# A four-layer graph network on one core: Chebyshev scan factors in PSUM, carries added through TensorE, merged softmax steps

## Chip, core and metric

The kernel runs on one core of a Trainium2 chip. The metric is the device time of one execution in microseconds. Engines are named as in the profile: PE (TensorE), DVE (VectorE), ACT (ScalarE), POOL (GpSimd) and SP (SyncE); SBUF and PSUM are the on-chip memories, and PSUM has eight banks.

## The reference, cut to what matters

A graph has N = 3125 nodes with 32 features and E = 53125 edges, which come sorted by destination `dst`. Four layers follow each other, each with a residual and a layer norm:

```python
x = layernorm(x + gat_gru(x))      # softmax over the incoming edges, 4 heads, then a GRU gate
x = layernorm(x + cheb_gatv2(x))   # two Chebyshev steps, then a softmax with 1 head
x = layernorm(x + spline(x))       # 16 tent weights per edge
x = layernorm(x + agnn(x))         # cosine softmax with 1 head
```

A Chebyshev step is a sum over incoming edges, and a softmax layer a weighted one:

```python
m   = (x * Dinv[:, None])[src]                       # gather rows of the sources
agg = segment_sum(m, dst) * Dinv[:, None]
mx  = segment_max(e, dst)                            # softmax layers: e is a logit per edge
ex  = exp(e - mx[dst]); den = segment_sum(ex, dst)
out = segment_sum(feat[src] * (ex / den[dst])[:, None], dst)
```

So there are five passes over all edges that gather, weight and sum rows: `gat`, `cheb0`, `cheb1`, `gatv2` and `agnn` (the spline layer has a loop of its own).

## The kernel before

**Layout.** The edges lie as 125 partitions x 425 in their sorted order, and a pass goes through them in 17 chunks of 25 columns. The nodes lie as 125 partitions x 25. A node's edges can go on from one partition into the next; what a partition's last node hands on is called its carry.

**A chunk of a pass.** Each of a chunk's 25 columns needs 125 rows of a table. PE gathers 14 of the columns (12 in gat): `gather_rows` (L726) multiplies one-hot matrices with the table, in 15 matmuls a column (5 lots of sources x 3 bf16 parts), into PSUM, two columns to a bank (`columns_ps`). DVE takes the results out in two halves, columns 0 to 5 and 6 to 13 (`take_half`): for each half five copies under a mask (L1149), each with a small `memset` of a tile `idle` ahead of it (L1148). PE may not write a half again until DVE has taken it. DVE also makes four of the five one-hots of a chunk (L1121), ACT the fifth (L922, L925). POOL gathers the other 11 columns (13 in gat) from DRAM, one indirect DMA a column (`gather`, L613).

When both sets of rows are there, ACT turns them so that a feature's 25 edges lie side by side (L984 in the Chebyshev passes), and writes the keep factors, which are 0 where a new node begins and 1 elsewhere (L987; in a softmax pass they are rescaling factors, L957). DVE multiplies with the weights (softmax passes, L1453), adds the carry of the chunk before (L1545, or L1463 for each head) and runs one segmented scan over 32 features x 25 edges (`scan_chunk`, L1400: one scan for each head of 33 features in the softmax passes). ACT turns the scan back (L993, L965), and SP stores it to DRAM.

In a softmax pass DVE also keeps a running maximum: `brk` (L1430) marks the new nodes, a copy carries the last maximum (L1433), and one scan for each head (L1435) follows; then come two differences and a sum (L1440 to L1443) for ACT's exponentials (L954).

**The end of a pass.** POOL waits until the last scan is stored (`scan_stored`), and gathers `local`, the value where each partition's first node ends (`mend_get_i`). In `mend` PE multiplies the partitions' last values with `carry_qp` (L753; in softmax passes L759, L764 and L770 with maxima and rescaling between them), and DVE adds the carry to `local` (`finish_sums`, L1521, or L1509). POOL scatters the sum, `mended`, back into the stored scan (`mend_put_i`, L616), waits for it to land, and gathers the last row of every node, 25 gathers in five blocks (`agg<-...,end_i`). DVE works on each block of five nodes a partition as it lands (`block_in`).

**What orders the work.** Each engine runs its own program in order, and semaphores tie them. Most engines run chunks 2 to 13 in a loop (`chunks`, L308), while DVE's softmax passes are written out. After its five copies DVE signals `half_taken`; after a chunk's last half it signals `rows_filled` by way of one more memset (L1539), for which ACT waits at L984. SP's queue loads edges and stores scans, and some of its waits count the scatters (`scattered`). A long list of slots between DVE's steps (`more_hots`, `settle`) says where the one-hots go.

## Time and profile before

| | us |
|---|---|
| three runs | 2582.41, 2583.98, 2584.41 (median 2583.98) |
| profiled execution, its own time | 2578.79 |
| its span in the profile | 2577.1 |

| engine | busy share of the span |
|---|---|
| PE, matmuls / weight loads | 75% / 66% |
| DVE | 71% |
| POOL | 67% |
| ACT | 35% |

| stage | from - to (us of the span) |
|---|---|
| setup | 0 - 107 |
| gat's loop, then its pass end and the GRU | 107 - 462, 462 - 541 |
| cheb0's loop, then its pass end | 541 - 810, 810 - 861 |
| cheb1's loop, then its pass end and the products for gatv2 | 861 - 1129, 1129 - 1221 |
| gatv2's loop, then its pass end | 1221 - 1527, 1527 - 1614 |
| spline layer | 1614 - 2195 |
| agnn's products, loop and pass end | 2195 - 2241, 2241 - 2523, 2523 - 2577 |

TensorE's granted clock is 0.877 on the mean. The stages were read off the timelines: a loop ends about where the last scan is stored. No engine is busy throughout, and different engines end the stages; a stage's time has to be read from the waits in it. Idle time of an engine that nothing waits for costs nothing.

### The profile page before, as it was taken

What the parts mean: (1) busy time and instruction counts of PE and PEld (TensorE: products, weight loads), DVE (VectorE), ACT (ScalarE), POOL (GpSimd) and SP (SyncE); (2) the same over time, 40 slices, a digit from 0 to 9 for tenths busy, and PEclk for the clock granted to TensorE, in tenths of its full rate; (3) what the DMA queues carried; (4) which work ended last, traced back from release to release, by engine and by line L of the source; (5) the groups of instructions that cost most, each with busy time, mean ns of one, the idle gap of its engine ahead of it and who ended that gap; (6) DMA issues with size and microseconds to landing.
All of it is one profiled execution on the core that took longest, in us unless ns stands there. A gap on an engine that the chain in (4) does not pass through costs nothing.

```text
span 2577.1 us, 51563 instructions
## 1 busy us (share of the span) xinstructions
PE 1930.1 (75%) x20425; PEld 1694.0 (66%) x20425; DVE 1825.0 (71%) x4970; ACT 895.8 (35%) x872; POOL 1736.5 (67%) x1625
## 2 busy tenths in 40 slices
PE   2778777269994699947788947588788878589990
PEld 2777777269994699946788942355455545589990
DVE  7699998355553355533899854588888888699975
ACT  0377775325443144422344425000000000144542
POOL 6777774447775677765566842677777776567773
...
DMA packets 83703, 194.91 MB, mean 76 GB/s; under 512 B 30960, under 2 KB 49816, under 8 KB 79746
## 3 DMA queue, kind: packets, MB, share of 16 engines
q1 hardware_dynamic: 31650, 139.14, 15.1%
...
## 4 chain that ended last, share of the span: by engine, by line
POOL 38%; DVE 23%; issue 19%; PE 10%; ACT 6%; DMA 5%; DVEq 0%; POOLq 0%; ACTq 0%; SPq 0%
POOL edges_d L613 18%; POOL rows L613 16%; PE ps L726 7%; DVE edges_d L1400 5%; POOL agg L613 3%; DVE edges_d L1329 3%; ACT scan L965 3%; DVE edges_d L1453 2%; DVE bigT L1400 2%; PE ps L883 2%; POOL starts_dram L616 2%; ACT edges_d L950 1%; DVE agg L1121 1%; DVE smallT L1121 1%; DMA starts_dram<-scan 1%
## 5 line engine op out<-in xcount | busy, mean ns | idle before, releaser
L726 PE MATMUL ps<-nodes,edges_d 125*128 125x160 bf16 x7140 | 502.7, 234 | 80.4 <-DVE nodes L1371 49.7
L726 PEld LDWEIGHTS ps<-nodes,edges_d 125*128 125x128 bf16 x7140 | 500.1, 99 | 82.9 <-DVE nodes L1371 49.8
L613 POOL DMA_INDIRECT edges_d<-tab_y_dram,attr x425 | 429.8, 1011 | 180.2 <-issue 129.2
L613 POOL DMA_INDIRECT rows<-tab_cheb_dram,src_i x374 | 409.4, 1095 | 148.4 <-issue 113.4
L726 PE MATMUL ps<-nodes,aggn 125*128 125x180 bf16 (+2 forms) x3546 | 394.8, 244 | 120.0 <-DVE rows L1149 62.9
L783 PE MATMUL ps<-edges_d,scan 125*125 125x480 bf16 x1700 | 361.3, 369 | 108.3 <-DVE edges_d L1813 108.3
L1149 DVE COPY_PREDICATED rows<-picks,ps 125x192 f32<-125x192 uint16 (+4 forms) x880 | 352.4, 402 | 79.3 <-issue 39.6
L783 PEld LDWEIGHTS ps<-edges_d,scan 125*125 125x125 bf16 x1700 | 226.2, 136 | 244.6 <-DVE edges_d L1813 113.5
L726 PE MATMUL ps<-nodes,agg 125*128 125x180 bf16 (+2 forms) x3564 | 336.0, 243 | 63.6 <-DVE rows L1149 63.6
L726 PEld LDWEIGHTS ps<-nodes,aggn 125*128 125x128 bf16 x3546 | 292.0, 101 | 126.5 <-issue 64.1
L726 PEld LDWEIGHTS ps<-nodes,agg 125*128 125x128 bf16 x3564 | 283.4, 101 | 69.5 <-DVE rows L1149 56.7
L613 POOL DMA_INDIRECT rows<-tab_dram,src_i x209 | 247.4, 1184 | 86.2 <-issue 59.1
L613 POOL DMA_INDIRECT rows<-tab_fsrc_dram,src_i x176 | 203.8, 1158 | 85.2 <-issue 50.6
L613 POOL DMA_INDIRECT rows<-tab_x_dram,src_i x176 | 195.3, 1109 | 70.3 <-issue 51.2
L1071 ACT ACTIVATE agg<-prod 125x160 bf16<-125x160 f32 x85 | 28.6, 337 | 543.1 <-DVE prod L1802 543.1
L726 PE MATMUL ps<-nodes,smallT 125*128 125x160 bf16 (+1 forms) x2214 | 202.8, 238 | 0.0
L984 ACT ACTIVATE bigT<-rows 125x800 f32<-125x800 f32 x34 | 54.2, 1593 | 331.0 <-DMA rows<-tab_cheb_dram,src_i 183.5
L726 PEld LDWEIGHTS ps<-nodes,smallT 125*128 125x128 bf16 x2214 | 169.0, 100 | 0.0
L1791 DVE TENSOR_TENSOR edges_d<-edges_d 125x640 f32<-125x640 f32 x85 | 71.0, 835 | 127.1 <-DMA edges_d<-tab_y_dram,attr 127.1
L1787 DVE TENSOR_SCALAR scan<-nodes,codes 125x625 bf16<-125x625 f16 x340 | 144.4, 441 | 0.0
L950 ACT ACTIVATE bigT<-rows 125x800 f32<-125x800 f32 x34 | 56.4, 1658 | 230.7 <-DVE rows L1149 225.6
L616 POOL DMA_INDIRECT starts_dram<-scat,start_i x75 | 77.8, 1038 | 78.6 <-DVE scat L1855 28.0
...
## 6 DMA issues: line engine op xcount, KB each, us to landing
...
edges_d<-tab_y_dram,attr POOLq DMA_INDIRECT x425, 2.6
...
```

The lines of the kernel that those rows point to most:

```text
L613: pool.indirect_dma_start(o, None, table, bass.IndirectOffsetOnAxis(index, 0)).then_inc(s, SLOT)
L616: pool.indirect_dma_start(table, bass.IndirectOffsetOnAxis(index, 0), rows_, None, bounds_check=last, oob_is_err=False).then_inc(scattered ...
L726: ins = pe.matmul(columns_ps[:, i, 0:PICKS * w], hots_[b][lot][:, i * NP:i * NP + P], parts_[:, part, at:at + PICKS * w], start=(lot == 0 ...
L783: ins = pe.matmul(ps[0:NP, lot, 0:PICKS * 3 * D], lot_hots[c][:, t, lot, :], picked[c][:, t, :, :].rearrange("p k c -> p (k c)"), start=(b ...
L950: nc.scalar.activation(z[b][:, at:at + D, :], r[:, :, 0:D].rearrange("p t f -> p f t"), ACT.Copy).then_inc(rows_flipped, 1)
L965: nc.scalar.activation(to, of, ACT.Copy).then_inc(rows_turned, 1)
L984: nc.scalar.activation(z[b], rows[0:NP, b, 0:L * D].rearrange("p (t c) -> p c t", c=D), ACT.Copy).then_inc(rows_used, 1)
L1149: ins = vec.copy_predicated(to[:, cols[0]:cols[-1] + 1, 0:w], over(picks[:, b, pick, cols[0]:cols[-1] + 1], w), columns_ps[0:NP, cols[0]:c ...
L1329: ins = vec.tensor_tensor_scan(ed[:, t0:t1, c], same_ps[:, t0:t1], ed[:, t0:t1, c], ed[:, t0 - 1, c:c + 1] if i else 0.0, ALU.mult, ALU.add)
L1400: ins = vec.tensor_tensor_scan(flat, keep[:, c:c + width, :].rearrange("p c t -> p (c t)"), flat, 0.0, ALU.mult, ALU.add)
L1787: vec.tensor_scalar(lot_hots[c][:, t, :, :].rearrange("p l c -> p (l c)"), nodes16[:, 0:LOTS * NP], codes[:, c, t:t + 1], None, ALU.is_equal)
L1791: vec.tensor_tensor(slot, slot, over(basis[:, bass.ds(t0 + c * LS, LS), :], D), ALU.mult)\
```

## The change

- **Chebyshev passes.** The keep factors no longer lie in SBUF but in PSUM banks 6 and 7 (`keeps_ps`), half of the features in each; ACT writes them in two activations, and DVE scans in two scans of 16 x 25 = 400 elements (`scan_sums`). To make room, PE's first half (six columns) lies three columns to a bank in banks 0 and 1 (`tight_ps`), the other eight two to a bank in banks 2 to 5. Matmuls and copies read their places from `column_ps` and `half_ps`.
- **Pass ends of cheb0, cheb1, gatv2 and agnn.** The scatter of `mended` goes, with the waits around it. The end rows are gathered straight behind the stored scan (in gatv2 and agnn behind the fetch of `local`, which stays for its maximum). The carry is added to the gathered rows: DVE spreads it over a partition's node columns (`carry_to_nodes`: one product of 25 x c elements), three f32 matmuls with `first_row_of` bring it to the right partition in PSUM banks 3 to 5, and `block_in` adds it to each block. In gatv2 and agnn the rows are rescaled first by factors for each node (`node_keep`, ten small operations), so a block takes four more operations. gat keeps its scatter.
- **Softmax passes.** All heads share one maximum scan, with a padded first element for each head; gat's four carry operations become two; the memsets of `idle` ahead of the copies go.
- **Setup.** An iota on POOL and some dozen small DVE operations make `first_row_of` and `first_col_of`; `no_carry_pq` is made at each pass end; `shift` moves into `bigT`. Counts of semaphores follow (SP waits for 2J+1 and 3J+1 scatters instead of 2J+3, 3J+4 and 3J+5).

The core of the diff (counts, tile declarations and renamed views are left out):

```diff
+        def mend_rows(c):
+            return tab[0:NP, :, :].rearrange("p j c -> p (j c)")[:, 0:J * c].rearrange("p (j c) -> p j c", c=c)
+        def mend_ps(m, c):
+            return ps[0:NP, 3 + m // 2, m % 2 * LS * c:(m % 2 + 1) * LS * c].rearrange("p (j c) -> p j c", c=c)
...
+        tight_ps = ps[:, 0:2, 0:3 * PICKS * D].rearrange("p b (s c) -> p b s c", s=3)
+        def column_ps(name, i):
+            if name not in ("cheb0", "cheb1"):
+                return columns_ps[:, i, 0:PICKS * GATHERED[name]]
+            if i < 6:
+                return tight_ps[:, i // 3, i % 3, :]
+            return columns_ps[:, i - 2, 0:PICKS * D]
+        def half_ps(name, half, cols, pick):
+            w = GATHERED[name]
+            if name not in ("cheb0", "cheb1"):
+                return columns_ps[0:NP, cols[0]:cols[-1] + 1, pick * w:(pick + 1) * w]
+            if half:
+                return columns_ps[0:NP, cols[0] - 2:cols[-1] - 1, pick * w:(pick + 1) * w]
+            return tight_ps[0:NP, :, :, pick * w:(pick + 1) * w]
+        HALF_D = D // 2
+        keeps_ps = [ps[0:NP, 6 + i, 0:HALF_D * L].rearrange("p (c t) -> p c t", t=L) for i in range(2)]
...
+                    if heads:
+                        gather(local[:, 0:C], scan_dram, mend_get_i[:, 0:1], local_in)
+                    if heads > 1:
+                        pool.wait_ge(vec_for_pool, vec_pool.up())
+                        scatter(scan_dram, mend_put_i[:, 0:1], mended[:, 0:C], E - 1)
+                        pool.wait_ge(scattered, put.at())
...
-                                        ins = pe.matmul(columns_ps[:, i, 0:PICKS * w],
+                                        ins = pe.matmul(column_ps(name, i),
...
+                def carry_to_nodes(c):
+                    pe.wait_ge(vec_for_pe, operand.up())
+                    for at in range(0, J, 2 * LS):
+                        n = min(2 * LS, J - at) * c
+                        ins = pe.matmul(ps[0:NP, 3 + at // (2 * LS), 0:n], first_row_of[:, :],
+                                        tab[0:NP, :, :].rearrange("p j c -> p (j c)")[:, at * c:at * c + n],
+                                        start=True, stop=True)
+                    ins.then_inc(pe_for_vec, 1)
...
+                        carry_to_nodes(D)
...
+                    if heads == 1:
+                        carry_to_nodes(MC)
...
-                        nc.scalar.activation(keep[:, :, 1:L],
-                                             samec[:, b, 1:L].unsqueeze(1).broadcast_to([NP, D, L - 1]),
-                                             ACT.Copy).then_inc(act_for_vec, 1)
+                        for part in keeps_ps:
+                            ins = nc.scalar.activation(part[:, :, 1:L],
+                                                       samec[:, b, 1:L].unsqueeze(1).broadcast_to([NP, HALF_D, L - 1]),
+                                                       ACT.Copy)
+                        ins.then_inc(act_for_vec, 1)
...
-                        vec.memset(idle[:, half * 8 + pick:half * 8 + pick + 1], 0.0)
-                        ins = vec.copy_predicated(to[:, cols[0]:cols[-1] + 1, 0:w],
-                                                  over(picks[:, b, pick, cols[0]:cols[-1] + 1], w),
-                                                  columns_ps[0:NP, cols[0]:cols[-1] + 1, pick * w:(pick + 1) * w])
+                        if name in ("cheb0", "cheb1"):
+                            vec.memset(idle[:, half * 8 + pick:half * 8 + pick + 1], 0.0)
+                        taken = to[:, cols[0]:cols[-1] + 1, 0:w]
+                        mask = picks[:, b, pick, cols[0]:cols[-1] + 1]
+                        if name in ("cheb0", "cheb1") and not half:
+                            taken = taken.rearrange("p (b s) c -> p b s c", s=3)
+                            mask = mask.rearrange("p (b s) -> p b s", s=3)
+                        ins = vec.copy_predicated(taken, over(mask, w), half_ps(name, half, cols, pick))
...
+                row_, col_, later = (place_of[:, i:i + 1] for i in range(3))
+                steps = cross[:, 0:NP]
+                again = cross[:, NP:2 * NP]
+                vec.tensor_scalar(row_, ends[:, 0:1], 1.0 / J, -(J // 2) / J, ALU.mult, ALU.add).then_inc(vec_done, 1)
+                settle()
...
+                vec.tensor_scalar(first_row_of[:, :], steps, row_, later, ALU.is_equal, ALU.mult)
+                vec.tensor_scalar(first_col_of[:, :], steps[:, 0:J], col_, None, ALU.is_equal)
...
+                def scan_sums(z, b):
+                    for i, part in enumerate(keeps_ps):
+                        flat = z[b][:, i * HALF_D:(i + 1) * HALF_D, :].rearrange("p c t -> p (c t)")
+                        ins = vec.tensor_tensor_scan(flat, part.rearrange("p c t -> p (c t)"), flat,
                                                      0.0, ALU.mult, ALU.add)
...
-                        vec.tensor_scalar(brk[:, :], same[:, bass.ds(t0, L)], -1.0, BIG, ALU.add, ALU.mult)
+                        vec.tensor_scalar(brk[:, 0:heads, 1:L + 1], same[:, t0:t0 + L].unsqueeze(1)
+                                          .broadcast_to([NP, heads, L]), -1.0, BIG, ALU.add, ALU.mult)
+                        vec.tensor_copy(padded_logit[:, 0:heads, 0:1], mrun[:, 1 - b, 0:heads, L:L + 1])
                         logits(r, t0)
-                        vec.tensor_copy(mrun[:, b, 0:heads, 0:1], mrun[:, 1 - b, 0:heads, L:L + 1])
-                        for h in range(heads):
-                            ins = vec.tensor_tensor_scan(mrun[:, b, h, 1:L + 1], brk[:, :], logit[:, h, :],
-                                                         mrun[:, 1 - b, h, L:L + 1], ALU.add, ALU.max)
-                        ins.then_inc(vec_done, 1)
+                        vec.tensor_tensor_scan(mrun[:, b, 0:heads, :].rearrange("p h t -> p (h t)"),
+                                               brk[:, 0:heads, :].rearrange("p h t -> p (h t)"),
+                                               padded_logit[:, 0:heads, :].rearrange("p h t -> p (h t)"),
+                                               0.0, ALU.add, ALU.max).then_inc(vec_done, 1)
...
-                        for h in range(heads):
-                            one_head = slice(h * HG, (h + 1) * HG)
-                            ins = vec.scalar_tensor_tensor(z[b][:, one_head, 0], z[1 - b][:, one_head, L - 1],
-                                                           rw[:, b, 0, h, 0:1], z[b][:, one_head, 0],
-                                                           ALU.mult, ALU.add)
-                        ins.then_inc(vec_done, 1)
+                        if heads == 1:
+                            vec.scalar_tensor_tensor(z[b][:, :, 0], z[1 - b][:, :, L - 1], rw[:, b, 0, 0, 0:1],
+                                                     z[b][:, :, 0], ALU.mult, ALU.add).then_inc(vec_done, 1)
+                        else:
+                            carried = mended[0:NP, 0:heads * HG].rearrange("p (h g) -> p h g", h=heads)
+                            vec.tensor_tensor(carried, z[1 - b][:, :, L - 1].rearrange("p (h g) -> p h g", h=heads),
+                                              over(rw[:, b, 0, 0:heads, 0], HG), ALU.mult).then_inc(vec_done, 1)
+                            settle()
+                            vec.tensor_tensor(zh[:, :, :, 0], zh[:, :, :, 0], carried, ALU.add).then_inc(vec_done, 1)
...
+                    if heads == 1:
+                        vec.tensor_copy(mended[0:NP, 0:HG], ps[0:NP, 6, 0:HG]).then_inc(vec_done, 1)
+                        settle()
+                        carry_to_nodes(mended[0:NP, 0:MC], MC)
+                        for m in range(J // LS):
+                            made = mend_ps(m, MC)
+                            vec.tensor_scalar(node_keep[:, 0, m * LS:(m + 1) * LS], made[:, :, HG + 2], -1.0, 1.0,
+                                              ALU.mult, ALU.add).then_inc(vec_done, 1)
+                        own.up(J // LS - 1)
+                        settle()
+                        for m in range(J // LS):
+                            js = slice(m * LS, (m + 1) * LS)
+                            vec.tensor_tensor(node_keep[:, 1, js], node_keep[:, 0, js], mend_ps(m, MC)[:, :, HG],
+                                              ALU.add).then_inc(vec_done, 1)
+                        own.up(J // LS - 1)
+                        settle()
+                        return
...
+                def carry_to_nodes(carry, c):
+                    vec.tensor_tensor(mend_rows(c), over(first_col_of[:, :], c),
+                                      carry.unsqueeze(1).broadcast_to([NP, J, c]), ALU.mult).then_inc(vec_for_pe, 1)
+                    vec.wait_ge(pe_for_vec, pe_n.up())
+                def block_in(m, heads=None):
                     vec.wait_ge(agg_in[m], agg_n.at())
+                    js = slice(m * LS, (m + 1) * LS)
+                    if heads == 0:
+                        vec.tensor_tensor(agg[0:NP, js, 0:D], agg[0:NP, js, 0:D], mend_ps(m, D), ALU.add)\
+                            .then_inc(vec_done, 1)
+                        settle()
+                    if heads == 1:
+                        vec.tensor_tensor(agg[0:NP, js, 0:HG], agg[0:NP, js, 0:HG], over(node_keep[:, 1, js], HG),
+                                          ALU.mult)
+                        vec.tensor_tensor(agg[0:NP, js, HG], agg[0:NP, js, HG], node_keep[:, 0, js], ALU.mult)\
+                            .then_inc(vec_done, 1)
+                        settle()
+                        vec.tensor_tensor(agg[0:NP, js, 0:HG], agg[0:NP, js, 0:HG], mend_ps(m, MC)[:, :, 0:HG], ALU.add)
+                        vec.tensor_tensor(agg[0:NP, js, HG], agg[0:NP, js, HG], mend_ps(m, MC)[:, :, HG + 1], ALU.add)\
+                            .then_inc(vec_done, 1)
+                        settle()
                 def finish_sums():
                     vec.wait_ge(pe_for_vec, pe_n.up())
-                    vec.wait_ge(local_in, local_n.up(SLOT))
-                    vec.tensor_tensor(mended[0:NP, 0:D], local[0:NP, 0:D], ps[0:NP, 6, 0:D], ALU.add)\
-                        .then_inc(vec_for_pool, 1)
+                    carry_to_nodes(ps[0:NP, 6, 0:D], D)
...
-                        scan_chunk(z, keep, b)
+                        scan_sums(z, b)
```

## Rows read from the trace of the kernel before

**Rows 1.** PE's timeline in cheb0's loop: start, us, instructions [idle before <-releaser]

```profile
541.91 162.75 PE L726 MATMUL ps<-nodes,edges_d 125*128 125x160 bf16 x2310 [21.35 <-issue]
705.59 14.70 PE L726 MATMUL ps<-nodes,edges_d 125*128 125x160 bf16 x210 [0.92 <-DVE rows L1149]
...
768.55 30.85 PE L726 MATMUL ps<-nodes,edges_d 125*128 125x160 bf16 x420 [2.09 <-DVE rows L1149]
```

**Rows 2.** PE's timeline in cheb1's loop, first and last of seven gaps

```profile
1008.61 14.70 PE L726 MATMUL ps<-nodes,edges_d 125*128 125x160 bf16 x210 [0.19 <-DVE rows L1149]
...
1100.79 14.68 PE L726 MATMUL ps<-nodes,edges_d 125*128 125x160 bf16 x210 [0.54 <-DVE rows L1149]
```

**Rows 3.** Groups by line and form: busy us, mean ns | idle before, releaser

```profile
L613 POOL DMA_INDIRECT rows<-tab_cheb_dram,src_i x374 | 409.4, 1095 | 148.4 <-issue 113.4 <-DMA tab_cheb_dram<-tab 34.9
...
L1716 DVE TENSOR_TENSOR prod<-prod,ps 125x800 f32<-125x800 f32 x17 | 16.8, 986 | 0.6
L1710 DVE TENSOR_TENSOR prod<-rows,edges_d 125x800 f32<-125x800 f32 x17 | 16.7, 983 | 0.0
```

**Rows 4.** Timelines of DVE and POOL at gatv2's start

```profile
1229.02 6.66 DVE L1329 TENSOR_TENSOR_SCAN edges_d<-ps,edges_d 125x75 f32<-125x75 f32 x32
...
1232.22 0.94 POOL L613 DMA_INDIRECT rows<-tab_fsrc_dram,src_i  x1 [0.30 <-issue]
```

**Rows 5.** Timelines of DVE and POOL, one cheb0 chunk; the last gather is cheb1's

```profile
559.59 0.44 DVE L1149 COPY_PREDICATED rows<-picks,ps 125x256 f32<-125x256 uint16 x1
...
566.74 1.82 DVE L1400 TENSOR_TENSOR_SCAN bigT<-bigT 125x800 f32<-125x800 f32 x1
...
566.99 2.32 POOL L613 DMA_INDIRECT rows<-tab_cheb_dram,src_i  x1 [0.30 <-issue]
...
570.13 0.37 DVE L1149 COPY_PREDICATED rows<-picks,ps 125x192 f32<-125x192 uint16 x1
...
1112.25 1.42 POOL L613 DMA_INDIRECT rows<-tab_cheb_dram,src_i  x1 [0.30 <-issue]
```

**Rows 6.** Timelines of DVE, ACT and POOL at the end of cheb0

```profile
801.96 0.06 DVE L1539 MEMSET idle<- 125x1 f32 x1
804.38 1.55 ACT L984 ACTIVATE bigT<-rows 125x800 f32<-125x800 f32 x1 [7.93 <-DMA rows<-tab_cheb_dram,src_i]
813.98 0.94 POOL L613 DMA_INDIRECT local<-scanD_dram,mend_get_i  x1 [11.10 <-DMA scanD_dram<-scan]
...
820.77 1.07 POOL L613 DMA_INDIRECT agg<-scanD_dram,end_i  x1 [1.38 <-DMA scanD_dram<-mended,mend_put_i]
```

**Rows 7.** Timelines of ACT and POOL at the end of cheb1

```profile
1122.68 1.54 ACT L984 ACTIVATE bigT<-rows 125x800 f32<-125x800 f32 x1 [7.94 <-DMA rows<-tab_cheb_dram,src_i]
1131.52 0.94 POOL L613 DMA_INDIRECT local<-scanD_dram,mend_get_i  x1 [10.36 <-DMA scanD_dram<-scan]
...
1137.44 0.96 POOL L613 DMA_INDIRECT agg<-scanD_dram,end_i  x1 [1.37 <-DMA scanD_dram<-mended,mend_put_i]
```

**Rows 8.** Timelines of POOL and PE at the end of gatv2

```profile
1530.46 0.94 POOL L613 DMA_INDIRECT local<-scan_dram,mend_get_i  x1 [18.34 <-DMA scan_dram<-scan]
...
1539.32 0.97 POOL L613 DMA_INDIRECT agg<-scan_dram,end_i  x1 [1.44 <-DMA scan_dram<-mended,mend_put_i]
...
1556.87 7.25 PE L883 MATMUL ps<-w_spl,smallT 32*125 32x512 f32 x8 [5.05 <-ACT smallT L900]
```

**Rows 9.** DVE's timeline in one chunk of gat

```profile
298.38 3.68 DVE L1453 TENSOR_TENSOR edges_d<-edges_d,ps 125x800 f32<-125x800 f32 x4 [0.58 <-ACT rw L954]
...
302.27 0.91 DVE L1463 SCALAR_TENSOR_TENSOR edges_d<-edges_d,rw 125x33 f32<-125x33 f32 x4
```

**Rows 10.** DVE's timeline at the end of agnn

```profile
2531.16 0.19 DVE L1509 TENSOR_TENSOR mended<-mended,ps 125x33 f32<-125x33 f32 x1 [0.72 <-PE ps L770]
2542.05 0.16 DVE L1880 TENSOR_TENSOR nodew<-agg,nodew 125x5 f32<-125x5 f32 x1 [10.70 <-DMA agg<-scan_dram,end_i]
...
2574.12 0.32 DVE L1592 TENSOR_TENSOR X<-X,nodew 125x160 f32<-125x160 f32 x1
```

85 lines of the change are left out of this document (55 added, 30 removed).

## The prediction

> **What bounds the kernel now.** I read the chain of waits first: it passes from stage to stage through different engines, so each stage has to be costed by itself. Then I read timelines of every engine, one chunk and one pass end per stage.
>
> In the two Chebyshev loops PE gathers by one-hot matmuls without a pause at first (cheb0's first eleven chunks take 162.75 us, 14.8 each); then it begins to wait for DVE's half-takes, in five gaps in cheb0, the first 0.92 us and the last 2.09, and in seven in cheb1, from 0.19 to 0.54 [rows 1, 2]. What makes DVE late is POOL. It issues 11 gathers a chunk, 374 in both loops with a mean of 1095 ns [rows 3]; an undisturbed one takes 0.94, with 0.30 of issue in front [rows 4], so 0.155 x 374 = 58 us are excess. 35 of the long gathers fall on a DVE scan, the first and the last shown: one begun just after a scan of 1.82 us takes 2.32 [rows 5]. Read one by one, those 35 hold 14.0 us of excess in cheb0 and 11.8 in cheb1; nearly all the rest falls beside the one-hot instructions, which stay. At the end of cheb0 DVE has taken its last half at 802.02, but ACT starts only at 804.38, on POOL's last rows [rows 6].
>
> At the pass ends POOL's 25 end-row gathers (1.25 us each) are the longest item. They begin only after fetch, mend, scatter-back and landing: 6.8 us after the fetch could have begun in cheb0 (813.98 to 820.77), 5.9 in cheb1, 8.9 in gatv2 [rows 6 to 8].
>
> In the gat loop DVE's weighted rows, scans and then ACT's copies form one closed ring: DVE waits 0.58 us for ACT's exponentials in a chunk [rows 9].
>
> **The change, part by part.**
>
> *Scan factors in PSUM.* While DVE ran 32 scans with one operand in PSUM for 6.66 us, POOL's gathers kept 0.94 [rows 4]. So I take off the whole scan excess: POOL's last rows come at 804.38 - 14.0 = 790.4 in cheb0 and at 1122.68 - 11.8 = 1110.9 in cheb1 [rows 6, 7]. PE's gaps then go: cheb0's add up to 5.1 us, and after the last, 420 matmuls took 30.85 instead of 2 x 14.70, 1.45 more; PE ends at 799.40 - 6.6 = 792.8 [rows 1]. DVE's last half ends 2.6 us behind PE (802.02 against 799.40) [rows 1, 6], so ACT starts at 795.4 instead of 804.38: 9.0 us. In cheb1 the gaps are 4.2 us; PE ends at 1111.3, ACT starts at 1113.9 instead of 1122.68: 8.8 us [rows 2, 7]. Late next is PE itself, at 14.6 to 14.8 us a chunk; POOL's 11 x 1.245 and 0.87 of stalls on one-hots make 14.6, just as long, so nothing beyond this is to be had.
>
> The new scan pair: 32 scans of 75 elements in 6.66 us are 2.8 ns an element [rows 4]; 800 in 1.82 are 2.3 [rows 5]. So 1.8 to 2.2 us; I take 2.0, since a larger scan spreads its fixed part. ACT's two half copies instead of one I put at 0.15 more (0 to 0.3). Both lie beside PE inside a loop: DVE's chain from the last half to the next half taken goes from 559.59 to 570.50, 10.9 us of PE's 14.7 [rows 1, 5]. At each loop's end they show, 0.3 us a pass. Net **-8.7 and -8.5**. Bounds: 0 (the scans hold POOL as before) and -9.0, -8.8.
>
> The tight layout of PE's first half changes no matmul. The split copies move the same elements; 0 to 0.1 us a piece, inside the 3.8 us of slack.
>
> *Carries through PE, cheb0 and cheb1.* The end-row gathers start when the scan is stored: 6.8 and 5.9 us earlier. The carry (one DVE product of 800, three f32 matmuls) runs while POOL gathers for 25 x 1.25 = 31 us. Its PE price: 4 products of 512 columns took 7.25 us, 3.5 ns a column [rows 8], so 800 cost 2.8, ready before the first five end rows. DVE adds one 160-element sum a block, 0.32 (the last of [rows 10]) and a gap, 0.4; one is exposed, behind the last block. **-6.4 and -5.5**; bounds 0.4 either way. Nothing queues behind POOL's dropped wait but these gathers.
>
> *Carries, gatv2 and agnn.* The local fetch stays (it gives the local maximum), the scatter goes: gathers start 1.25 us behind the fetch, at 1531.7 instead of 1539.3 [rows 8], 7.6 earlier; agnn is alike. But DVE gets a longer way to its first block. In agnn: the mended row at 2531.16 + 0.19, a product of 900 (0.98 for 800 [rows 3], so 1.1), 900 f32 columns (3.2), ten factors of five elements (0.06 to 0.16 each, 1.1), with gaps: 2537.0 instead of 2542.05, so 5.05 earlier [rows 10]. Each block then gets two 165-element and two 5-element operations, 0.95 us. agnn's blocks are already DVE's bound: from 2542.05 to 2574.44 five take 6.5 us each, over the 6.24 that five gathers need [rows 10]. All five additions count: -5.05 + 4.75 = **-0.3**. In gatv2 the same steps bring the first block 5.2 to 5.5 us earlier; PE's spline products, which wait through ACT's copy for the second block, start as much before 1556.87 [rows 8]; the fourth block, with one addition of 0.95 more ahead of it, leaves **-4.6**. Bounds: gatv2 -7.6 to 0, agnn -5 to +3.
>
> *Merged softmax steps.* In gat's ring only one piece changes: four carries of 0.91 us with gap become two of 0.29 with a wait between, 0.65 against 0.94 [rows 9]: 0.29 x 17 = **-4.9**. The merged maximum scan, the wider break row and the dropped memsets lie in the time in which DVE waits for ACT anyway: nothing. Bounds 0 and -6. In gatv2 and agnn a memset of 0.06 us (one like it: the first of [rows 6]) goes before each of ten copies a chunk; it lies inside the copy before it, so I take 0; were each worth its 0.06 in some 20 chunks that DVE bounds, 12.
>
> *Setup.* A dozen small DVE operations, some 2 us, stand before the counting; PE's first matmul waits for the zero-fill of a table and its last one-hot, so they are covered. If that cover were gone, +2. I take 0.
>
> **Sum**: -8.7 - 6.4 - 8.5 - 5.5 - 4.6 - 0.3 - 4.9 = -38.9, say 39 us, against a profiled span of 2577.1 (own time 2578.79, 5.2 under the median of the runs). Set against the median: 2583.98 - 39 = **2545 us**.
>
> One rule speaks against the change. The product of gatv2's logits that reads PSUM took 986 ns at 800 elements, the one before it out of SBUF 983 [rows 3]: 3 ns. The Trainium skill's VectorE: DVE Perf Modes (its section on the TRN2 errata) gives a fixed part of 120 cycles for a PSUM source against 58 for SBUF, an estimated 0.065 us for each new PSUM reader. By it the twenty or so new readers of the agnn tail and a few in the others would cost some 2.5 us, and the sum would be 2547.5; the row says it would not.
>
> **Rivals.** (1) *The scans go on holding POOL*, because what delays a gather is not the factors' place. Then both loops stay as they are and 39 - 17.2 = 21.8 remain: 2562. For it: the scans of rows 4 step through their tile with a stride, the new ones run contiguously. Against it: every one of their neighbours stayed near 0.94. A page would have it so: the Trainium skill's SBUF — State Buffer (Who interferes with whom) infers that a two-input DVE operation takes only the read interface while a DMA's descriptors need the write interface, by which such a scan would not stall a gather at all, and its place could not matter. The trace does not agree: 2.32 us on a scan [rows 5]. 8%.
> (2) *The carry chain becomes the bound of the tails.* If the carry's matmuls and node factors take twice my 5.4 us, gatv2 and agnn start their blocks later than reckoned, 0.8 and +5.1 instead of -4.6 and -0.3: 2555. For it: the tails are DVE-bound already. Against: the f32 price is measured. 8%.
> (3) *Slower:* the DVE chain takes PE's place in the Chebyshev loops, because scans or copies with PSUM are slow. A chunk now lasts 15.1 us on the mean (541.91 to 799.40, 17 of them); the other parts save 21.8, so this decides from 34 chunks x 0.64, a chunk of 15.8, which means a chain of 10.9 + 4.9. ACT's factor copy and the scan, some 2.7 now, would have to triple: 16.4 a chunk, +44 - 21.8, 2606. Against: rows 4 price the scan 20% up at most. 4%.
> (4) *The carry brings nothing because POOL is not the gate of the pass ends*: then 24 of 39 remain: 2560. Against: DVE idles until the first end rows land [rows 10]. 3%.
>
> **The numbers.** Forecast 77%, rivals 8, 8, 4, 3. The forecast's own bounds reach from 2531 (memsets worth their length, parts at their better ends) to 2555; with rival 1, and setup uncovered, at 2564 the range is 2531 to 2564. 0.2%, 5.2 us, is about what a measurement can tell from no change. Faster 92%; same 4% (the loops worse by what rival 3 needs to break even); slower 4%.
>
> **What would show it.** Chebyshev gathers that fall on scans at 0.94 instead of 1.4 to 2.3, and a mean near 1.02; PE gapless to the end of both loops; end-row gathers directly behind the stored scan; agnn's blocks at 7.5 us instead of 6.5; gat's chunk shorter by 0.3. Wrong would be: gathers still stretched; gaps in PE on DVE's halves; blocks that wait for the carry's matmuls for more than 3 us.

## The result, and the profile after

The changed kernel takes 2538.99 us (median; 2537.42 to 2542.16), against 2583.19 for the kernel before (four runs of each; the three runs shown ahead of the prediction are among them): a ratio of 0.9832 with a 95% interval of 0.9815 to 0.9849, or 44 us. Its profiled execution took 2538.81 us with a span of 2537.1, 40.0 us under the span of before.

From the page of the changed kernel, the span, the busy times and the engines' shares of the chain of waits:

```profile
span 2537.1 us, 51142 instructions
PE 1942.4 (77%) x20449; PEld 1701.2 (67%) x20449; DVE 1836.8 (72%) x4471; ACT 899.3 (35%) x906; POOL 1704.3 (67%) x1620
...
PE 28%; POOL 25%; DVE 24%; issue 13%; ACT 6%; DMA 4%; ACTq 0%; POOLq 0%; DVEq 0%; SPq 0%
```

The same line of the chain in the kernel before:

```profile
POOL 38%; DVE 23%; issue 19%; PE 10%; ACT 6%; DMA 5%; DVEq 0%; POOLq 0%; ACTq 0%; SPq 0%
```

POOL is busy 32 us less, the others about as long as before. What changed is who ends the stages: PE holds 28% of the chain instead of 10, POOL 25 instead of 38. To see where, I cut the span at instructions that both traces have: each pass's first gather matmul, and the first matmul of each pass end (the carry in the Chebyshev passes, the maxima in the softmax passes). The times are differences of such starts in PE's timelines. "Before, again" is the run e10_before_again below.

| stage (us) | before | before, again | after | measured change | predicted |
|---|---|---|---|---|---|
| setup | 73.1 | 72.7 | 72.7 | -0.4 | 0 |
| gat's loop | 383.6 | 384.0 | 382.8 | -0.7 | -4.9 |
| gat's end and the GRU | 85.3 | 84.9 | 84.8 | -0.4 | 0 |
| cheb0's loop | 268.7 | 267.3 | 257.8 | -10.9 | -8.7 |
| cheb0's end | 50.3 | 50.1 | 43.9 | -6.4 | -6.4 |
| cheb1's loop | 268.0 | 267.5 | 258.8 | -9.2 | -8.5 |
| cheb1's end | 69.5 | 69.6 | 64.2 | -5.3 | -5.5 |
| gatv2's loop | 327.6 | 327.6 | 322.9 | -4.7 | 0 |
| gatv2's end | 109.3 | 109.2 | 105.3 | -3.9 | -4.6 |
| spline layer | 585.4 | 591.5 | 589.5 | +4.1 | 0 |
| agnn's loop | 300.7 | 300.9 | 299.2 | -1.5 | 0 |
| agnn's end | 55.7 | 55.0 | 55.2 | -0.5 | -0.3 |

Between the two profiles of the kernel before, the spline layer moves by 6.1 us, cheb0's loop by 1.4, and no other stage by more than 0.7.

**The Chebyshev loops.** PE's timeline in cheb0 and cheb1, where before five and seven gaps stood [rows 1, 2], has one row for each loop:

```profile
540.36 248.72 PE L763 MATMUL ps<-nodes,edges_d 125*128 125x160 bf16 x3570 [21.36 <-issue]
...
842.09 249.72 PE L763 MATMUL ps<-nodes,edges_d 125*128 125x160 bf16 x3570 [39.14 <-DVE nodes L1448]
```

All 17 chunks run without a gap. Groups by line and form (busy us, mean ns | idle before, releaser):

```profile
L648 POOL DMA_INDIRECT rows<-tab_cheb_dram,src_i x374 | 382.0, 1022 | 148.8 <-issue 113.3 <-DMA tab_cheb_dram<-tab 35.4
...
L1488 DVE TENSOR_TENSOR_SCAN bigT<-ps,bigT 125x400 f32<-125x400 f32 x68 | 63.6, 977 | 1.2
...
L1034 ACT ACTIVATE bigT<-rows 125x800 f32<-125x800 f32 x34 | 54.3, 1596 | 302.8 <-DVE idle L1673 302.8
```

The gathers went from a mean of 1095 ns [rows 3] to 1022, and read one by one, none that falls on a scan is stretched any more: all that begin during one take 0.94 or 0.95 us. What excess is left lies beside the one-hots (L1121 before, L1173 after), which read one tensor and one column out of SBUF: 60 gathers that begin during one take more than 1.0 us, 28 us over 0.943 in both loops together, where it was 29 before. Two scans of 400 take 1.87 us where one of 800 took 1.82 [rows 5]. ACT now waits only for DVE's report that the last half is taken (L1673), and no longer for POOL's rows.

**The pass ends.** The end of cheb0 after the change, timelines of ACT, PE, POOL and DVE in order of time (start, us, instruction [idle before <-releaser]):

```profile
791.79 1.56 ACT L1034 ACTIVATE bigT<-rows 125x800 f32<-125x800 f32 x1 [8.04 <-DVE idle L1673]
...
799.92 3.03 PE L786 MATMUL ps<-tab,first_row_of 125*125 125x320 f32 x6 [1.15 <-DVE tab L1630]
801.39 0.94 POOL L648 DMA_INDIRECT agg<-scanD_dram,end_i  x1 [14.60 <-DMA scanD_dram<-scan]
...
809.09 0.32 DVE L1639 TENSOR_TENSOR agg<-agg,ps 125x160 f32<-125x160 f32 x1 [0.90 <-DMA agg<-scanD_dram,end_i]
```

The end rows' gathers are released by the stored scan itself and no longer by the scattered sum [rows 6]. The carry is through PE at 802.95, before the first five end rows have come, and each addition waits for its rows. In agnn the order is the other way round (the last row is the fifth block's):

```profile
2487.59 0.94 POOL L648 DMA_INDIRECT agg<-scan_dram,end_i  x1 [0.30 <-issue]
...
2493.47 3.36 PE L786 MATMUL ps<-tab,first_row_of 125*125 125x360 f32 x6 [1.42 <-DVE tab L1630]
2496.87 0.44 DVE L1614 TENSOR_SCALAR diag<-ps 125x5 f32<-125x5 f32 x5 [3.46 <-PE ps L786]
2497.35 0.44 DVE L1620 TENSOR_TENSOR diag<-diag,ps 125x5 f32<-125x5 f32 x5
2497.82 0.33 DVE L1643 TENSOR_TENSOR agg<-agg,diag 125x165 f32<-125x165 f32 x1
...
2527.19 0.33 DVE L1643 TENSOR_TENSOR agg<-agg,diag 125x165 f32<-125x165 f32 x1
```

The first block is not released by a DMA: its last row has landed at 2495.70, and DVE comes to it straight from the carry, after 3.46 us of waiting for PE and 0.95 of node factors. The blocks then follow each other every 7.34 us on the mean (2497.82 to 2527.19, four times), where it was 6.50.

### The profile page after: what moved, and what is told of

It reads as the page before. It is cut to its first block, busy times and chain, and to the rows that moved or that the text cites. A ratio compares the mean times of both kernels' runs of the same rounds, so it can differ in the third digit from the quotient of the medians.

```text
span 2537.1 us, 51142 instructions
## 1 busy us (share of the span) xinstructions
PE 1942.4 (77%) x20449; PEld 1701.2 (67%) x20449; DVE 1836.8 (72%) x4471; ACT 899.3 (35%) x906; POOL 1704.3 (67%) x1620
## 4 chain that ended last, share of the span: by engine, by line
PE 28%; POOL 25%; DVE 24%; issue 13%; ACT 6%; DMA 4%; ACTq 0%; POOLq 0%; DVEq 0%; SPq 0%
PE ps L763 25%; POOL edges_d L648 18%; DVE edges_d L1479 5%; POOL rows L648 3%; DVE rows L1207 3%; DVE edges_d L1406 3%; ACT scan L1015 3%; POOL agg L648 2%; DVE edges_d L1542 2%; PE ps L933 2%; POOL starts_dram L651 2%; DVE bigT L1479 1%; ACT edges_d L1000 1%; DVE agg L1173 1%; DMA starts_dram<-scan 1%
## 5 line engine op out<-in xcount | busy, mean ns | idle before, releaser
L648 POOL DMA_INDIRECT rows<-tab_cheb_dram,src_i x374 | 382.0, 1022 | 148.8 <-issue 113.3
## 6 DMA issues: line engine op xcount, KB each, us to landing
starts_dram<-scan SPq DMA_DIRECT2D x2, 3400.0 KB, 13.9
```

Source lines behind the costliest of these rows:

```text
L648: pool.indirect_dma_start(o, None, table, bass.IndirectOffsetOnAxis(index, 0)).then_inc(s, SLOT)
```

## The experiments

Each is the changed kernel with one edit, if nothing else is said; loops and ends are cut as in the table above. The diffs show the heart of an edit; "..." marks what is left out. The kernel before, run beside each group of experiments, had medians between 2582.84 and 2585.15 us, so times less than 3 us apart are not told apart here.

**e1_sbuf_factors and e2_one_sbuf_scan: what freed POOL?** The factors' place and the length of the scan changed together, so each needs a run of its own. e1 puts the factors back into SBUF and keeps the two scans:

```diff
-                    for i, part in enumerate(keeps_ps):
+                    for i, part in enumerate([keep[:, i * HALF_D:(i + 1) * HALF_D, :] for i in range(2)]):
```

(the same for ACT's two activations and the first column's memset). e2 has one activation and one scan of 800 as well:

```diff
-                        scan_sums(z, b)
+                        scan_chunk(z, keep, b)
```

> The changed kernel with its keep factors in SBUF again; the two scans of 400, ACT's two activations and the tight layout stay. Theory (what held POOL is that both operands of the scan lie in SBUF): both Chebyshev loops, from the first gather matmul to the carry matmul, go back from 257.8 and 258.8 us to about 268 each, gathers on scans take 1.4 to 2.3 us again, the time is about 2560 us (+20). Rival (two shorter scans let POOL through, wherever the factors lie): the loops stay at 258 to 260, at most +3 us.

> As e1_sbuf_factors, but with one scan of 800 and one activation as in the kernel before; only the tight layout of PE's columns is left of this part. Theory: within 3 us of e1_sbuf_factors, about 2560 us, loops of 268 us, so that the layout is worth nothing by itself. Rival (the split or the layout carries part of the gain): the two kernels differ by over 5 us, or the loops stay clearly under 268.

**e8_psum_one_scan** is the fourth corner: the factors in PSUM, as 800 elements in a row over banks 6 and 7, and one scan:

```diff
-                    for i, part in enumerate(keeps_ps):
-                        flat = z[b][:, i * HALF_D:(i + 1) * HALF_D, :].rearrange("p c t -> p (c t)")
-                        ins = vec.tensor_tensor_scan(flat, part.rearrange("p c t -> p (c t)"), flat,
...
+                    flat = z[b].rearrange("p c t -> p (c t)")
+                    ins = vec.tensor_tensor_scan(flat, keep_flat, flat, 0.0, ALU.mult, ALU.add)
```

> The changed kernel with its factors in PSUM, but as 800 elements in a row over both banks, read by one scan as long as that of the kernel before. Theory (a PSUM operand lets POOL through however long the scan): gathers on scans stay at 0.94 us, the loops at 258 to 259 us, time within 3 us of the changed kernel. Rival (only the length of a scan counts): gathers on scans at 1.4 to 2.3 us and loops of 268 us each, time about 2559 us.

| | one scan of 800 | two scans of 400 |
|---|---|---|
| factors in SBUF | e2: loops 268.9 and 268.3, 2561.25 us | e1: loops 258.9 and 258.6, 2542.28 us |
| factors in PSUM | e8: loops 257.7 and 259.0, 2542.72 us | changed kernel: 257.8 and 258.8, 2538.99 us |

The Chebyshev gathers and scans in e1, e2 and e8, groups by line and form, with the line of e1 for ACT's wait:

```profile
L648 POOL DMA_INDIRECT rows<-tab_cheb_dram,src_i x374 | 389.1, 1040 | 149.2 <-issue 113.4 <-DMA tab_cheb_dram<-tab 35.4 <-DMA scanD_dram<-scan 0.3
...
L1488 DVE TENSOR_TENSOR_SCAN bigT<-bigT 125x400 f32<-125x400 f32 x68 | 63.7, 978 | 1.2
...
L1034 ACT ACTIVATE bigT<-rows 125x800 f32<-125x800 f32 x34 | 54.3, 1597 | 303.5 <-DVE idle L1673 289.6 <-DMA rows<-tab_cheb_dram,src_i 13.9
```

```profile
L648 POOL DMA_INDIRECT rows<-tab_cheb_dram,src_i x374 | 410.3, 1097 | 149.0 <-issue 113.1 <-DMA tab_cheb_dram<-tab 35.5 <-DMA scanD_dram<-scan 0.3
...
L1477 DVE TENSOR_TENSOR_SCAN bigT<-bigT 125x800 f32<-125x800 f32 x34 | 62.0, 1825 | 1.2
```

```profile
L650 POOL DMA_INDIRECT rows<-tab_cheb_dram,src_i x374 | 383.3, 1025 | 148.6 <-issue 113.1 <-DMA tab_cheb_dram<-tab 35.1 <-DMA scanD_dram<-scan 0.3
...
L1489 DVE TENSOR_TENSOR_SCAN bigT<-ps,bigT 125x800 f32<-125x800 f32 x34 | 62.0, 1823 | 1.3 <-DVE bigT L1679 0.2
```

My theory for e1 fell: the loops did not go back, and its rival had them right. e2 shows that the gain is in this part, and that the tight layout, which e2 keeps, is worth nothing by itself. e8 shows that the place in PSUM is enough: a scan as long as before leaves the gathers alone. And e1 shows that the split is enough for the time. One chunk of e1 and one of e2, timelines of DVE and POOL:

```profile
564.68 1.87 DVE L1488 TENSOR_TENSOR_SCAN bigT<-bigT 125x400 f32<-125x400 f32 x2
564.86 1.57 POOL L648 DMA_INDIRECT rows<-tab_cheb_dram,src_i  x1 [0.30 <-issue]
```

```profile
564.61 1.82 DVE L1477 TENSOR_TENSOR_SCAN bigT<-bigT 125x800 f32<-125x800 f32 x1
564.88 2.31 POOL L648 DMA_INDIRECT rows<-tab_cheb_dram,src_i  x1 [0.31 <-issue]
```

A gather that begins 0.2 to 0.3 us into the first scan takes 0.63 us more than 0.94 where the scans are halves, and 1.37 where it is one. Read one by one, it is held to the end of the scan in which it begins: in the kernel before, in e2 and in e1 32 gathers each begin during a scan, and every one of them ends 0.75 us behind that scan's end. So in e1 gathers are still stretched, by 3.7 and 2.6 us a loop instead of 14.0 and 11.8, but POOL then needs 11 x (1.040 + 0.303) = 14.8 us a chunk, close to PE's 14.6. PE's timeline in e1 has no gap in either loop; only ACT waits 13.9 us for POOL's rows, which it does not in the changed kernel. The two means do the same work twice here. Whether the 3 to 4 us between e1 or e8 and the changed kernel (for e8 under 3 were expected) are theirs stays open: the spline stage, in which they do not differ, is 2.5 and 1.1 us longer in their profiles.

**e3_scatter_back** has the pass ends of before in cheb0, cheb1, gatv2 and agnn:

```diff
-                    if heads:
-                        gather(local[:, 0:C], scan_dram, mend_get_i[:, 0:1], local_in)
-                    if heads > 1:
-                        pool.wait_ge(vec_for_pool, vec_pool.up())
...
+                    gather(local[:, 0:C], scan_dram, mend_get_i[:, 0:1], local_in)
+                    pool.wait_ge(vec_for_pool, vec_pool.up())
+                    scatter(scan_dram, mend_put_i[:, 0:1], mended[:, 0:C], E - 1)
+                    pool.wait_ge(scattered, put.at())
```

> The changed kernel with the pass ends of before in cheb0, cheb1, gatv2 and agnn: fetch, scatter, landing, then end rows. Theory: the ends go back to 50.3, 69.5, 109.3 and 55.7 us, together +16 us, about 2555 us, and nothing else moves. Rival (the ends had another gate, and the gain there comes from something else): under +8 us.

Measured: 2557.41 us, and ends of 50.4, 69.3, 109.5 and 55.0 us. The first three are back where they were, together 15.8 us; agnn's, which the change had moved by 0.5, stays. Nothing else moved by more than the spline stage does between profiles. The carries are worth what the ends show.

**e4_max_scans, e5_memsets, e6_four_carries, e11_old_steps: the softmax steps, one by one and together.** e4 has a maximum scan for each head again, e5 a memset ahead of every copy, e6 gat's four carries, e11 all three. gatv2 and agnn have one head, so they have one scan either way; what e4 moves there is the small copy ahead of it.

```diff
-                        vec.tensor_tensor_scan(mrun[:, b, 0:heads, :].rearrange("p h t -> p (h t)"),
...
+                        for h in range(heads):
+                            ins = vec.tensor_tensor_scan(mrun[:, b, h, 1:L + 1], brk1, logit[:, h, :],
+                                                         mrun[:, 1 - b, h, L:L + 1], ALU.add, ALU.max)
```

```diff
-                        if name in ("cheb0", "cheb1"):
+                        if True:
                             vec.memset(idle[:, half * 8 + pick:half * 8 + pick + 1], 0.0)
```

```diff
-                        if heads == 1:
-                            vec.scalar_tensor_tensor(z[b][:, :, 0], z[1 - b][:, :, L - 1], rw[:, b, 0, 0, 0:1],
...
+                        for h in range(heads):
+                            one_head = slice(h * HG, (h + 1) * HG)
+                            ins = vec.scalar_tensor_tensor(z[b][:, one_head, 0], z[1 - b][:, one_head, L - 1],
...
```

> The changed kernel with one maximum scan for each head and the narrow break row, as before; carries and memsets stay as changed. Theory (gat is a ring of DVE's weighted rows, scans and ACT; gatv2 and agnn are mostly bound by DVE): gat's loop within 1 us, with DVE's wait for the exponentials down from 19.6 to about 13 us; gatv2's loop +1 to +2.5, agnn's 0 to +2; time +1 to +4 us. Rival (gat is bound by all that DVE does): gat's loop +6 us, 0.35 a chunk.

> The changed kernel with a memset of idle ahead of each of the ten copies of a chunk in the softmax passes too. Theory (gatv2's loop, which got 4.7 us shorter and of which the maximum scan gives back 1.7, is bound by DVE, and each memset delays the copy behind it by 10 ns or more): gatv2's loop +2 to +3 us, agnn's +0 to +3, gat's +0 to +2; time +2 to +7 us. Rival (a memset lies inside the copy before it): all three loops within 1 us.

> The changed kernel with gat's four carry operations of 33 elements instead of the two of 132. Theory (the two take 0.41 and 0.43 us with a wait between, the four 0.91 together, so the ring is as long as before): gat's loop within 1 us of 382.8, time within 3 us of the changed kernel. Rival (two operations are shorter by 0.29 us in the ring, as was reckoned): gat's loop +4.9 us.

> The changed kernel with all softmax steps as before: maximum scans for each head, four carries in gat, memsets ahead of all copies. Theory (together they are worth what gatv2's loop shows, each of them little): gatv2's loop back to 326 to 328 us, agnn's to 300 to 302, gat's 383 to 385; time +5 to +9 us on the changed kernel. Rival (gatv2's gain has another cause, such as the pass end of cheb1 ahead of it): gatv2's loop stays at 323 to 325.

| | gat's loop | gatv2's loop | agnn's loop | time |
|---|---|---|---|---|
| changed kernel | 382.8 | 322.9 | 299.2 | 2538.99 |
| e4_max_scans | 384.1 | 324.6 | 300.8 | 2544.88 |
| e5_memsets | 383.5 | 323.1 | 300.6 | 2542.81 |
| e6_four_carries | 382.7 | 323.5 | 299.0 | 2540.96 |
| e11_old_steps | 385.5 | 326.9 | 300.9 | 2548.15 |

Two expectations failed by their sizes: e4 costs 5.9 us, not 1 to 4, and e5 gives back 0.2 us in gatv2, not 2 to 3, but 1.4 in agnn, which the rival had not either. e6 and e11 came within half a microsecond of theirs. Where the softmax steps are untouched (e1, e2, e3, e7, e8, e9, e12), gatv2's loop lies between 322.7 and 324.9 and agnn's between 298.9 and 300.3. So in gatv2 the 1.7 us of e4 are not clear of the spread and the 0.2 of e5 are nothing; e11's 326.9 lies clear of it. In agnn e4, e5 and e11 stand 0.3 to 0.6 us above it.

A shorter stretch says more. In the first nine chunks of these two loops, from the first `brk` to the tenth in DVE's timeline, DVE waits for nothing but ACT's exponentials; in the rest of the loop it also waits for gathered rows. agnn's first and tenth `brk` in the changed kernel and in e11:

```profile
2222.43 0.18 DVE L1518 TENSOR_SCALAR brk<-same 125x25 f32<-125x25 f32 x1
...
2372.08 0.18 DVE L1518 TENSOR_SCALAR brk<-same 125x25 f32<-125x25 f32 x1
```

```profile
2233.91 0.18 DVE L1519 TENSOR_SCALAR brk<-same 125x25 f32<-125x25 f32 x1
...
2384.87 0.18 DVE L1519 TENSOR_SCALAR brk<-same 125x25 f32<-125x25 f32 x1
```

| us | agnn, nine chunks | gatv2, nine chunks | gatv2, rest of the loop | excess of its gathers there |
|---|---|---|---|---|
| before; before, again | 150.91; 150.91 | 165.73; 165.75 | 120.4; 120.5 | 18.4; 18.8 |
| changed kernel | 149.65 | 164.38 | 117.3 | 15.5 |
| steps untouched, eight runs with e6 | 149.58 to 149.68 | 164.34 to 165.03 | 117.1 to 118.6 | 15.3 to 16.9 |
| e4_max_scans | 150.26 | 164.77 | 118.5 | 17.6 |
| e5_memsets | 150.75 | 165.17 | 116.5 | 14.9 |
| e11_old_steps | 150.96 | 165.85 | 119.4 | 18.4 |

(A gather's excess is its time over 0.943 us.) In the nine chunks e11 gives back all of the 1.3 us that the change had won in each loop. In agnn, where the spread is 0.1 us, 0.6 come back with e4 and 1.1 with e5's ninety memsets, 12 ns each. The other 3.1 of gatv2's 4.7 us lie in the rest of the loop, and there the excess of POOL's gathers went down by 2.9 us and comes back with e11. The length of that rest roughly follows the excess through the runs, so I put this part down to POOL's rows; which of DVE's operations hold the gathers there was not taken apart.

In gat e6 decides: four carries are as good as two. The lines of gat's loop in the changed kernel say why, ahead of them the two of the kernel before (groups by line and form within the loop: busy us, mean ns | idle before, releaser):

```profile
L1453 DVE TENSOR_TENSOR edges_d<-edges_d,ps 125x800 f32<-125x800 f32 x64 | 58.9, 982 | 12.9 <-ACT rw L954 12.9
...
L1463 DVE SCALAR_TENSOR_TENSOR edges_d<-edges_d,rw 125x33 f32<-125x33 f32 x64 | 14.5, 292 | 0.6
```

```profile
L1542 DVE TENSOR_TENSOR edges_d<-edges_d,ps 125x800 f32<-125x800 f32 x64 | 58.9, 983 | 19.6 <-ACT rw L1004 19.6
...
L1558 DVE TENSOR_TENSOR edges_d<-edges_d,mended 125x132 f32<-125x132 f32 x16 | 6.9, 428 | 0.6
L1555 DVE TENSOR_TENSOR mended<-edges_d,rw 125x132 f32<-125x132 f32 x16 | 6.6, 410 | 0.6
```

Two operations on 132 elements take 0.41 and 0.43 us, not 0.29 each. And the rest that DVE saves in gat comes back as a longer wait for ACT's exponentials, 19.6 us instead of 12.9: that wait is where the merged maximum scan went, for in e4 it is 14.1 again. What gat's loop itself differs by in e4 and e11, 1.3 and 2.7 us, lies mostly ahead of its first `brk` (35.1 and 36.1 us behind the first gather matmul, 33.9 in the changed kernel).

**e10_before_again** is the kernel before, unchanged.

> The kernel before, profiled once more, to see how far its stages spread between two profiles. Theory (the differences over 3 us between the two kernels' stages are theirs): gatv2's loop within 1 us of 327.6, the spline stage within 2 us of 585.4, the Chebyshev loops within 1 us of 268.7 and 268.0. Rival (the 4.7 us of gatv2's loop and the 4 us lost in the spline stage are spread): one of them moves by 3 us or more.

Measured: 2583.34 us; gatv2's loop 327.6 as in the first profile, the Chebyshev loops 267.3 and 267.5, but the spline stage 591.5 instead of 585.4. The Chebyshev loops are 1.4 and 0.5 us shorter, where at most 1 was expected. So gatv2's 4.7 us belong to the change, and the 4 us that the spline stage seemed to lose don't: that stage spreads by 6 us between two profiles of one kernel. Its loop is bound by POOL, 425 gathers with a mean of 1011 ns in one profile of the kernel before and 1026 in the other; 15 ns x 425 are 6.4 us. The gathers meet DVE's operations in another rhythm.

**e7_block_carries: a better version of the pass ends.** The carry of gatv2 and agnn goes through PE block by block, with factor and addend in one row of 68 values, and a block takes two operations:

```diff
...
+                        vec.scalar_tensor_tensor(agg[0:NP, js, 0:C1], made[:, :, C1:BC], 1.0, agg[0:NP, js, 0:C1],
+                                                 ALU.add, ALU.mult).then_inc(vec_done, 1)
+                        settle()
+                        vec.tensor_tensor(agg[0:NP, js, 0:C1], agg[0:NP, js, 0:C1], made[:, :, 0:C1], ALU.add)\
+                            .then_inc(vec_done, 1)
```

> A version of the changed kernel for gatv2 and agnn: the carry and the rows' factors go through PE block by block (five products of 340 elements and five matmuls of 340 columns, into banks 3 to 7), so that DVE can start with the first block, and a block takes two operations instead of four. Theory (in the changed kernel the first block waits for the whole carry chain, 3.46 us for PE and 1 us of small factors, while its rows have landed): agnn's end from 55.2 to about 51.7 us, gatv2's from 105.3 to about 102.5, time about 2533 us. Rival (the blocks wait for their rows in any case): agnn's end -1.2 us from the shorter blocks, gatv2's 0.

Measured: 2534.37 us; agnn's end 51.4, gatv2's 103.7, where 51.7 and 102.5 were expected. DVE's and PE's timelines in agnn:

```profile
2489.20 2.20 DVE L1618 TENSOR_TENSOR bigT<-first_col_of,mended 125x340 f32<-125x340 f32 x5
2489.77 5.12 PE L825 MATMUL ps<-bigT,first_row_of 125*125 125x340 f32 x10 [0.83 <-DVE bigT L1618]
2492.41 0.34 DVE L1643 SCALAR_TENSOR_TENSOR agg<-ps,agg 125x170 f32<-125x170 f32 x1 [1.00 <-PE ps L825]
...
2499.56 0.33 DVE L1643 SCALAR_TENSOR_TENSOR agg<-ps,agg 125x170 f32<-125x170 f32 x1
```

From the pass end's first matmul (2479.22) to the first block are 13.2 us instead of 15.9 (2481.95 to 2497.82). So in the changed kernel the carry chain did hold the first block, by the 2.12 us between its rows' landing (2495.70) and its start. In e7 the rows land at 2492.38, 0.03 us ahead of the block, so there they are its gate, although the row above names PE.

**e9_short_picks and e12_short_adds: the same lever elsewhere.** If shorter operations let POOL through, the spline layer should show it most. e9 is e7 with one operation of 1200 elements split in three, e12 is e9 with an add of 320 elements split in two:

```diff
-                        vec.tensor_tensor(picked[c].bitcast(I32),
...
+                        for t in range(0, LS, 2):
+                            ts = slice(t, min(t + 2, LS))
+                            ins = vec.tensor_tensor(picked[c][:, ts].bitcast(I32),
...
```

```diff
-                        vec.tensor_tensor(slot[:, :, 0:2, :], slot[:, :, 0:2, :], slot[:, :, 2:4, :], ALU.add)\
-                            .then_inc(vec_done, 1)
+                        for i in range(2):
+                            ins = vec.tensor_tensor(slot[:, :, i, :], slot[:, :, i, :], slot[:, :, 2 + i, :], ALU.add)
+                        ins.then_inc(vec_done, 1)
```

> e7_block_carries with one more split: in the spline layer the and of 1200 int32 elements (1.41 us) becomes three of 480, 480 and 240. Theory (what holds a gather is the rest of a DVE operation with both operands in SBUF, so shorter operations hold it for less, and the spline loop is bound by POOL at 425 gathers of 1.02 + 0.30 us): the gathers' excess beside this line, 10.3 us of 31 in the changed kernel, falls by about half, the spline stage goes from 589 to about 584 us, time about 2529 us. Rival (DVE, whose chain gets 0.1 us longer a slot, bounds the loop, or the gathers only meet the next operation instead): 588 to 592 us as before, time about 2534.

> e9_short_picks with the spline layer's add of 320 elements in two of 160. In e9 one gather a slot, 1.21 to 1.27 us long, begins while this add runs; 16.6 of the remaining 19 us of excess lie beside it. Theory (a gather that begins during an operation waits for the end of that operation, so that half the length gives half the wait or less): the excess beside the adds falls to under 8 us, the spline stage from 576.7 to 562 to 570 us, time 2506 to 2514 us. Rival (the gather, set free earlier, makes a later one meet the next operation, a one-hot of 0.38 us that stays whole): the excess moves to that line and the stage stays within 4 us of 576.7.

Measured: e9 takes 2520.30 us, a ratio to the kernel before of 0.9751 (0.9737 to 0.9764), the best of all; its spline stage takes 576.7 us. e12 takes 2553.40, with a spline stage of 606.0: not nothing, as the rival had it, but 29 us worse. The spline gathers in the changed kernel, in e9 and in e12, groups by line and form:

```profile
L648 POOL DMA_INDIRECT edges_d<-tab_y_dram,attr x425 | 433.9, 1021 | 183.5 <-issue 129.2 <-DMA tab_y_dram<-edges_d 54.3
```

```profile
L649 POOL DMA_INDIRECT edges_d<-tab_y_dram,attr x425 | 420.9, 990 | 182.2 <-issue 129.2 <-DMA tab_y_dram<-edges_d 53.0
```

```profile
L649 POOL DMA_INDIRECT edges_d<-tab_y_dram,attr x425 | 450.1, 1059 | 182.2 <-issue 129.2 <-DMA tab_y_dram<-edges_d 53.0
```

A slot of e9 and one of e12 in the timelines of DVE and POOL:

```profile
1800.69 0.48 DVE L1929 TENSOR_TENSOR edges_d<-edges_d 125x320 f32<-125x320 f32 x1
1800.78 1.21 POOL L649 DMA_INDIRECT edges_d<-tab_y_dram,attr  x1 [0.30 <-issue]
```

```profile
1801.06 0.55 DVE L1930 TENSOR_TENSOR edges_d<-edges_d 125x160 f32<-125x160 f32 x2
1801.10 1.09 POOL L649 DMA_INDIRECT edges_d<-tab_y_dram,attr  x1 [0.30 <-issue]
...
1802.05 0.67 DVE L1918 TENSOR_SCALAR scan<-nodes,codes 125x625 bf16<-125x625 f16 x2
1802.49 1.52 POOL L649 DMA_INDIRECT edges_d<-tab_y_dram,attr  x1 [0.30 <-issue]
1802.64 0.32 DVE L1939 TENSOR_TENSOR agg<-prod,agg 125x160 bf16<-125x160 f32 x1
1802.87 0.32 DVE L1940 TENSOR_TENSOR prod<-prod,agg 125x160 f32<-125x160 f32 x1
```

In e9 the excess beside the line that was split (each gather is put down to the DVE operation that it lies beside longest) goes from 11.3 us (e7) to 0.5, further down than by the half that was expected. What is left, 19.5 of 20.2 us, belongs to gathers that begin while the whole add runs, one in most slots, with a mean of 1.21 us. In e12 such a gather takes 1.05, as the theory had it, but so the next one begins earlier, during one of DVE's one-hots: 84 of these take 1.22 to 1.52 us and hold 41.3 of the 49.3 us of excess. The rival had the later gather right and its price too low: it let that gather wait for a one-hot of 0.38 us, while each of the 84 ends 0.81 to 0.83 us behind the end of an f32 operation that follows the one-hot (61 behind L1940, 23 behind the next, L1943).

## Why the prediction was right, and where it was not

The forecast was 2545 us, 39 less; it came to 2538.99, 44 less, inside the range. In the profiles, where the sum was made, it is 38.9 against 40.0, and that closeness is in part luck: gat's missing gain and the 4.1 us that the spline layer spread by stand against gains that were not forecast in the other loops. Point by point:

**The Chebyshev loops** (-17.2 forecast, -20.1 measured). What was to be seen came: unstretched gathers on scans, a mean of 1022 ns, no gaps, DVE's last half 2.6 us behind PE (789.08 to 791.69), ACT released by DVE. Mis-sized was PE's own end, which came 2.2 us earlier than reckoned in cheb0 (248.72 us behind its start, not 250.9) and 0.6 in cheb1. Part of that is not the change's: cheb0's first chunk took 17.34 us in the profile of before, at a mean granted clock of 0.83 (1.00 in the ten behind it), and 16.16 after, at 0.89; but it took 16.18, at 0.89, in the second profile of the kernel before too. In cheb1 the first chunk went the other way, from 16.59 to 17.16. The rest is that I took off the gaps alone: from its first matmul to the next chunk's a chunk takes 14.52 us without a gap and 15.61 with one of 0.92, so a gap costs 0.17 more than itself, and cheb0 had five, cheb1 seven. The scan pair (1.87 us, taken as 2.0) and ACT's two halves (0.88 us together) added 0.1 a loop's end, not 0.3.

**The reason behind them** was half the truth. That a PSUM operand lets POOL through is shown by e8. But rows 4, on which I rested it, were short scans as well as PSUM scans, and I did not price the split on its own: e1 has the whole gain of the loops with its factors in SBUF. Rival 1, that the place does not matter, is wrong for the gathers (e8); for the time the place turned out not to be needed, but the loops did not stay as they were, as that rival had it (e1). The rule that stood beside that rival can be judged too: the Trainium skill's SBUF — State Buffer (Who interferes with whom) says that a DVE instruction with at most one SBUF input, outside the two-port modes, does not contend with GpSimd, and e8's 800-element scan agrees (0.94 to 0.95 us for the gathers that begin during it). Its inference that `tensor_tensor` takes only the read interface, so that descriptor generation goes on, is neither borne out nor refuted by the 2.31 us of a gather on e2's scan, and the prediction was too quick to say that the trace does not agree: these gathers also read their indices from a tile in SBUF (`src_i`), and no run here separates that reading from the making of descriptors.

**The carries** were forecast best: -6.4, -5.5, -4.6 and -0.3 against -6.4, -5.3, -3.9 and -0.5. In agnn the two terms that cancel each other were each a little smaller than reckoned: the first block came 4.75 us earlier instead of 5.05, and a block grew by 0.84 instead of 0.95; -4.75 + 5 x 0.84 = -0.55. That -0.5 is inside the 0.7 by which this end moves between profiles. In gatv2 PE's first spline product begins 5.5 us earlier, as reckoned (25.27 us behind the pass end's first matmul instead of 30.79), but its last ends 4.0 earlier (82.27 instead of 86.23): the later blocks lose 1.6 us, not 0.95. One sign that was named for being wrong did come, blocks that wait for the carry's matmuls for more than 3 us: DVE waits 3.46 in agnn. My sum held 3.2 for these matmuls, so that the sign was set too close to the forecast itself. Rival 2, that the carry chain bounds the tails, is how agnn stands, only that its price was in my sum already; e7 takes 3.8 us out of it there and 1.7 in gatv2.

**The softmax steps** are the step that failed, in both directions, and the two errors nearly cancelled. For gat I took each merged carry at the 0.29 us of a 33-element operation; with 132 elements they take 0.41 and 0.43, and the gain of 4.9 us was nothing (e6). For gatv2 and agnn I let the maximum scan and the memsets lie in DVE's wait for ACT, as in gat, and took them at nothing. Groups by line within gatv2's loop, before and after:

```profile
L1453 DVE TENSOR_TENSOR bigT<-bigT,ps 125x800 f32<-125x800 f32 x17 | 16.8, 989 | 6.9 <-ACT rw L954 6.9
```

```profile
L1542 DVE TENSOR_TENSOR bigT<-bigT,ps 125x800 f32<-125x800 f32 x17 | 16.8, 989 | 6.9 <-ACT rw L1004 6.9
```

That wait is 0.41 us a chunk, the same before and after, so it absorbed nothing. In the nine chunks in which DVE waits for nothing else its savings show whole, 1.3 us in each loop. The other 3.1 of gatv2's 4.7 us came, as the gathers' excess through the runs has it, by a way that the sum did not have at all: POOL's gathers were held less, and the rows for which DVE waits late in that loop came earlier. e11 gives back 4.0 of the 4.7 and all of agnn's 1.5.

**PSUM readers.** The rule that I weighed against the change, a larger fixed part for a PSUM source (the Trainium skill's VectorE: DVE Perf Modes, on the TRN2 errata), stays unseen here for operations with one operand in each place: 977 ns for a scan of 400 with its factors in PSUM, 978 in e1 with both operands in SBUF.
